# A fused attention, pooling and feed-forward kernel: finer waits and moved set-up in groups two to six, and a first group prepared by three engines

## The chip, the cores and the metric

The kernel runs on one core of a Trainium2 chip. The metric is the device time of one execution in microseconds (us). Three runs of the kernel before gave a median of 279.13 us (278.16 to 279.15).

## What is computed

The input is x, 64 sequences of 64 tokens with 256 features (4096 tokens). Cut to what matters:

```python
# 1. rotation of x by a ** dt and cos, sin of f * dt (one scalar dt per sequence)
xr = stack([c * x0 - s * x1, s * x0 + c * x1])
# 2. linear attention, 16 heads of 16, keys layer-normed, decay gamma = sigmoid(log_gamma)
q, k, v = split(xr @ W_qkv.T);  k = layernorm(k)
S = gamma * S + outer(v_t, k_t);  y_t = S q_t
x = x + y @ W_o.T
# 3. pooling: softmax over masked scores tanh(x W1 + b1) v; one of three masks per sequence
x_p = softmax(masked(scores)) @ x / count
# 4. feed-forward with fake-quantized activations and weights (I = 704)
scale_w = max(abs(w), axis=1) / 127
x = x + down(quant(silu(gate(quant(x_p))) * up(quant(x_p))))
```

The weight scales (largest entry of a row over 127, and its inverse) and the sigmoid of two clip factors are the set-up that the change moves.

## The kernel before

The 4096 tokens are cut into eight groups of 512 (`for g in range(G)`, g from 0 to 7). I call them groups 1 to 8. Each engine has its own hand-written instruction list, with counting semaphores between them; nothing is reordered, so an instruction that waits holds up everything behind it on its engine. After the eight groups, the feed-forward part follows for all tokens (from about 205 us); the change does not touch it.

**One group.** TensorE (block `pe`, line 872 on) computes `scores(g, 0)`, `project_v(g)`, the transposed rows of the group before (`x1_rows`), `scores(g, 1)`, then `weights_turn` (line 964 on; it transposes softmax weights of two groups before), `hidden_layer`, `pool_tokens`, `score_rows`, then the first `values_pair`, the K projection of the next group, `squares`, half of the Q projection, the other `values_pair`s, `sums_turn` (line 1061; it transposes the sums of squared keys), the other half of Q, and `project` for four token blocks, which multiplies y by the output weights. In the first two groups of tokens (c < TURNED) `weights_turn` waits for `p_ok`, that is for normalized softmax weights; later it waits for the exponents only.

VectorE (block `dve`, line 1332 on) runs per group: `decays(g, 0)` (L1460, four products of scores and decay factors), `scale_v` (L1530), `decays(g, 1)`, `softmax_scores` (L1540 to L1542), `largest_rows` (L1560), `softmax_weights` (line 1545 on: a sum L1547, a product of four numbers L1548, a reciprocal L1550 or L1552, and in the first two blocks a 128x256 product L1555), `y_odd(g, 0)` (L1475), `sums_copy(g + 1)` (L1418), `low_y(g, 0)` (L1480), then in groups 3 to 5 the weight scales (`gu_scales`, `down_scales`, lines 1443 to 1456: largest entries L1444, a scaling L1445, a reciprocal L1446) and in group 3 the clip factors (L1599, L1600), `y_odd(g, 1)`, `low_y(g, 1)`, `newton(g + 1)` (L1514 to L1519, eleven dependent steps for an inverse square root), and the two `residual`s (L1468). The first group's `sums_copy(1)` comes after `low_y(0, 1)`.

ScalarE copies results out of PSUM: `next_x` (L662), `x1_columns` (L667), `k_copies` (L638, L639), `y_even` (L651), `y_high` (L656), `q_copies` (L644). A half of y goes: values on TensorE, `y_even` on ScalarE, `y_odd` on VectorE, `y_high` on ScalarE, `low_y` on VectorE, `project` on TensorE.

GpSimd does, per group, `low_x(g + 1)` (L531, two 128x512 products, right after `next_x`), the rotation of the group after that (`rotate`, L517 to L525, six 128x512 products) and the masks (`allowed`, L546 to L551).

**Waits of the values projection.** `project_v(g)` of groups 2 to 8 waits, before anything, for the Newton steps and the first residual:

```python
if g:
    pe.wait_ge(rs_ok, g + 1)
    pe.wait_ge(x1_done, 2 * g - 1)
```

**The start.** The first group is prepared apart. VectorE computes the angles (L1357 to L1369), ScalarE their sines (L615, L616), GpSimd the powers `a_pow` (L504, first for 8 columns, then for 24). VectorE multiplies both to `cs` (L1385, L1386), rotates the first group in six 128x512 products (L1391 to L1401), centres the key weights (L1407), rounds them (L1408, `wT`, with the rest `wT_lo` in L1410), takes `xT_lo` (L1413) and the rests of the other weights (`low_weights`, L1422), multiplies the later columns of `cs` (L1426, L1427) and writes the decay exponents in sixteen operations (L1437), whose `dec_arg` releases ScalarE's exponential (L728) and GpSimd's `rotate(1)`. ScalarE computes exp and log for the decay rates (L620, L716), with two table loads, and rounds the query weights (L618). TensorE turns `cs` (L1108) ahead of the first half of Q, `squares(0, ...)`, and `sums_turn(0)`. `keep_clock` (L1030) are matmuls on constants without use for the result.

## Time and profile before

| what | us |
|---|---|
| median of three runs | 279.13 |
| profiled execution | 279.3 |
| its span | 277.6 |
| TensorE busy (share of the span) | 255.3 (92%) |
| VectorE busy | 232.6 (84%) |
| ScalarE busy | 180.6 (65%) |
| GpSimd busy | 145.2 (52%) |
| granted TensorE clock, all slices | 1.00 |

Busy time is what an engine spent on instructions; the span begins with the first and ends with the last instruction of the execution. In rows of the trace, PE is TensorE, PEld its weight loads, DVE VectorE, ACT ScalarE, POOL GpSimd. A row gives the start, the length and, in square brackets, how long the engine was idle before it and what it waited for. Matrix multiplications in FP32 count as two instructions there.

### The profile page before, as it was taken

What the parts mean: (1) busy time and instruction counts of PE and PEld (TensorE: products, weight loads), DVE (VectorE), ACT (ScalarE), POOL (GpSimd) and SP (SyncE); (2) the same over time, 40 slices, a digit from 0 to 9 for tenths busy, and PEclk for the clock granted to TensorE, in tenths of its full rate; (3) what the DMA queues carried; (4) which work ended last, traced back from release to release, by engine and by line L of the source; (5) the groups of instructions that cost most, each with busy time, mean ns of one, the idle gap of its engine ahead of it and who ended that gap; (6) DMA issues with size and microseconds to landing.
All of it is one profiled execution on the core that took longest, in us unless ns stands there. A gap on an engine that the chain in (4) does not pass through costs nothing.

```text
span 277.6 us, 8491 instructions
## 1 busy us (share of the span) xinstructions
PE 255.3 (92%) x3545; PEld 176.0 (63%) x3545; DVE 232.6 (84%) x501; ACT 180.6 (65%) x316; POOL 145.2 (52%) x140
## 2 busy tenths in 40 slices
PE   5898999988998899899899999998889999998995
PEld 5767769657877777777777886885634434433331
DVE  4999869479699878978987786787888999999994
ACT  2775481552467647768748547527689999847991
POOL 6939595990593278059339533003212679850570
PEclk9999999999999999999999999999999999999999
DMA  5990504400900530194084033040009489000167
GB/s 164 336 275 3 153 0 151 159 2 13 293 5 2 190 117 2 35 291 43 0 302 62 2 129 84 2 138 22 0 0 200 113 219 348 35 0 0 72 256 280
DMA packets 30311, 31.20 MB, mean 112 GB/s; under 512 B 12929, under 2 KB 20673, under 8 KB 30273
## 3 DMA queue, kind: packets, MB, share of 16 engines
q1 hardware_dynamic: 30272, 30.66, 37.2%
q8 instruction: 28, 0.46, 0.7%
q14 instruction: 11, 0.08, 0.1%
HBM read 19.48 MB, written 8.42 MB: 100 GB/s over the span
## 4 chain that ended last, share of the span: by engine, by line
PE 45%; DVE 32%; ACT 13%; issue 6%; DMA 1%; POOL 1%; DVEq 0%; ACTq 0%
PE psum L879 11%; PE psum L1271 6%; PE psum L904 4%; DVE yT_lo L1480 4%; PE psum L1290 3%; DVE psum L1475 3%; PE psum L986 3%; ACT silu L842 2%; PE psum L961 2%; ACT silu L824 2%; PE psum L1030 2%; DVE arena L1468 2%; PE psum L942 2%; PE psum L1023 2%; DVE arena L1651 2%
## 5 line engine op out<-in xcount | busy, mean ns | idle before, releaser
L1460 DVE TENSOR_TENSOR arena<-psum,xq_mem 128x512 f32<-128x512 f32 x64 | 39.7, 682 | 7.0 <-PE psum L904 7.0
L531 POOL TENSOR_TENSOR xT_lo<-arena,xT 128x512 fp32r<-128x512 f32 x14 | 18.0, 1308 | 46.1 <-ACT xT L662 46.1
L1271 PE MATMUL psum<-xq_mem,guT 128*128 128x512 bf16 x152 | 33.9, 380 | 0.2
L662 ACT ACTIVATE xT<-arena 128x512 fp32r<-128x512 f32 x14 | 8.1, 623 | 29.5 <-PE psum L879 26.0
L1271 PEld LDWEIGHTS psum<-xq_mem,guT 128*128 128x128 bf16 x152 | 14.4, 98 | 19.4 <-DVE arena L1651 1.8
L1662 DVE TENSOR_REDUCE h_max<-arena 128x1 f32<-128x1024 f32 (+1 forms) x24 | 25.9, 1123 | 0.2
L824 ACT ACTIVATE silu<-psum,gu_x 128x1024 f32<-128x1024 f32 (+1 forms) x24 | 24.4, 1025 | 2.1 <-PE psum L1271 1.1
L879 PE MATMUL psum<-wT,xT 128*128 128x256 f32 x64 | 17.3, 293 | 4.8 <-DVE arena L1468 4.8
L1475 DVE SCALAR_TENSOR_TENSOR psum<-psum,pmask,arena 128x256 f32<-128x256 f32 x28 | 12.3, 485 | 10.0 <-ACT arena L651 10.0
L904 PE MATMUL psum<-arena 32*64 32x128 f32 x1024 | 19.3, 278 | 1.1 <-issue 1.1
L644 ACT ACTIVATE arena<-psum,pmask 128x512 f32<-128x512 f32 x32 | 20.1, 684 | 0.1
L1290 PE MATMUL psum<-arena,dT 128*128 128x512 bf16 x80 | 18.9, 381 | 1.2 <-DVE arena L1721 0.6
L919 PE MATMUL psum<-arena 64*32 64x128 f32 x1024 | 19.5, 274 | 0.4 <-DVE arena L1460 0.4
L879 PE MATMUL psum<-woT,yT 128*128 128x256 f32 x64 | 17.2, 291 | 1.0 <-ACT yT L656 0.9
L919 PEld LDWEIGHTS psum<-arena 64*32 64x32 f32 x1024 | 13.9, 106 | 6.3 <-issue 6.3
L904 PEld LDWEIGHTS psum<-arena 32*64 32x64 f32 x1024 | 15.5, 131 | 3.7 <-issue 2.6
L598 POOL CAST arena<-silu 128x1024 bf16<-128x1024 int8 (+1 forms) x9 | 9.6, 1095 | 14.3 <-DVE silu L1716 13.1
L656 ACT ACTIVATE yT<-psum 128x256 fp32r<-128x256 f32 x28 | 10.7, 387 | 9.3 <-DVE psum L1475 9.2
L879 PE MATMUL psum<-wT_lo,xT 128*128 128x256 f32 x64 | 16.7, 282 | 0.0
L879 PE MATMUL psum<-woT_lo,yT 128*128 128x256 f32 x64 | 16.6, 282 | 0.0
L517 POOL TENSOR_TENSOR arena<-xin,cs_rows 128x512 f32<-128x512 f32 x7 | 9.4, 1342 | 13.8 <-DMA cs_rows<-cs_dram 9.0
L546 POOL TENSOR_TENSOR xq_mem<-kind,xq_mem 128x256 f32<-128x256 f32 x8 | 5.1, 635 | 21.8 <-DVE arena L1542 21.8
(251 smaller groups left out, 734.1 us busy)
## 6 DMA issues: line engine op xcount, KB each, us to landing
arena<-in_x SPq DMA_DIRECT2D x9, 512.0 KB, 3.8
x_dram<-arena SPq DMA_DIRECT2D x8, 512.0 KB, 4.1
pooled<-x_dram SPq DMA_DIRECT2D x8, 512.0 KB, 5.3
out<-pooled SPq DMA_DIRECT2D x15, 256.0 KB, 2.2
xin<-in_x_t SPq DMA_DIRECT2D x7, 512.0 KB, 4.5
cs_rows<-cs_dram SPq DMA_DIRECT2D x12, 256.0 KB, 5.2
pooled<-in_w_qkv_t SPq DMA_DIRECT2D x3, 256.0 KB, 4.9
pooled<-in_w_down SPq DMA_DIRECT2D x1, 704.0 KB, 7.4
```

What stands on the lines that cost most here:

```text
L531: pool.tensor_tensor(xT_lo[:, k, :], xrotT[:, k, :], xT[:, k, :].bitcast(F32), ALU.subtract).then_inc(xl_ok, 1)
L644: act.activation(qblk[:, c, odd, :], Q_BANK[c][:, :], ACT.Identity, scale=pmask[:, odd:odd + 1]).then_inc(q_ok, 1)
L824: act.activation(silu_tile(n, v)[:, a:], gate_bank(v)[:, a:], ACT.Silu, scale=gu_x[:, 0, v:v + 1]).then_inc(silu_ok, 1)
L879: return pe.matmul(o, w(k), x(k), start=start, stop=stop) if stationary_w else pe.matmul(o, x(k), w(k), start=start, stop=stop)
L904: mm = pe.matmul(bank[S_BANK[r]][S * b:S * b + S, p * P:p * P + P], kT[rows, c, t:t + S], qblk[rows, c, :, t:t + S], start=True, stop=True)
L919: last = pe.matmul(Y_BANK[half][b][32 * r:32 * r + 32, at_y:at_y + P], v_rows[rows, p, at_v:at_v + 32], dec[rows, c, r, p, :], start=True, ...
L1271: mm = pe.matmul(in_order(o[:, 512 * half:512 * half + 512], 2 * n + half), gT[i][:, v, c, :], xq_rows(2 * n + half, c), start=(c == 0), s ...
L1290: return pe.matmul(o, dT[:, c, v, :], hid_q[:, U * n + 2 * v + half, 0:512], start=first, stop=last)
L1460: dve.tensor_tensor(dec[:, c, r, :, :], bank[S_BANK[r]].rearrange("q (n k) -> q n k", n=PP), two_heads, ALU.mult).then_inc(dec_done, 1)
L1475: dve.scalar_tensor_tensor(o, y_psum(b, half, 1), pmask[:, 1:2], y_rows(b, half), ALU.mult, ALU.add).then_inc(y_ok, 1)
L1480: dve.tensor_tensor(y_part(yT_lo, b, half), y_full(g, b, half), y_part(yT, b, half).bitcast(F32), ALU.subtract).then_inc(yl_ok, 1)
L1662: dve.tensor_reduce(h_max[:, n, v:v + 1], hid_step(n, v), AX.X, ALU.max, apply_absolute_value=True).then_inc(hm_done, 1)
```

## The change

**Groups two to six.** `project_v` waits for `rs_ok` before its first half and for the first residual only before its second. `newton` can run in two parts: four steps after `low_y(g, 0)`, seven after `low_y(g, 1)`. `sums_turn` moves ahead of the second `values_pair`s, and `sums_copy` of groups 2 to 7 ahead of `y_odd(g, 0)`; in group 1 it moves ahead of `low_y(0, 1)`. `softmax_weights` is cut: the sum stays (`softmax_sums`), the rest goes to the next group, between `scale_v` and `decays(g, 1)`. The largest weight entries are taken one group earlier, between `sums_copy` and `y_odd(g, 0)` (groups 2, 3 and 4); the scales follow in groups 3, 4 and 5, and the clip factors in group 6, all of them between `scale_v` and `decays(g, 1)`.

**The first group.** ScalarE takes the absolute value, exp and log of the decay rates at once, ahead of the sines, and multiplies one half of each rotation product in eight 128x128 pieces; VectorE adds the other half in eight pieces, each with its own wait. GpSimd centres the key weights and rounds those of q and v. The decay exponents are two 128x512 products, from a table in which GpSimd has put 1e20 where no decay is wanted. GpSimd's `rotate(1)` no longer waits for `dec_arg`. The exponential of the decays is cut in two, between `q_copies`. TensorE turns `cs` after the first half of Q, and runs fewer `keep_clock` matmuls.

```diff
@@ TensorE @@
@@ def project_v(g)
                 pe.wait_ge(kT_ok, DC * g + DC)
-                if g:
-                    pe.wait_ge(rs_ok, g + 1)
-                    pe.wait_ge(x1_done, 2 * g - 1)
                 for j in (0, 1) if g else (1, 0):
-                    if g == 0 and j == 0:
-                        pe.wait_ge(rs_ok, 1)
+                    if j == 0:
+                        pe.wait_ge(rs_ok, g + 1)
+                    elif g:
+                        pe.wait_ge(x1_done, 2 * g - 1)
@@ the start
-            keep_clock(2, bank[3][:, 0:P], ident[:, :], ident[:, :])
...
-                keep_clock(4, bank[3][:, 0:P], ident[:, :], ident[:, :])
+                keep_clock(1, bank[3][:, 0:P], ident[:, :], ident[:, :])
...
+            pe.wait_ge(wl_ok, 1)
+            project_x(0, Q_BANK, 0, 0, q_mm)
             pe.wait_ge(cs_ok, 2)
             pe.wait_ge(csr_ok, 2)
             pe.transpose(bank[4][0:2 * NPAIR, 0:P], cs[:, :, :].rearrange("p k n -> p (k n)"), ident[:, :]).then_inc(cs_tr, 1)
-            pe.wait_ge(wl_ok, 1)
-            project_x(0, Q_BANK, 0, 0, q_mm)
@@ the groups
+                    if g:
+                        sums_turn(g + 1)
                     values_pair(1, 0)
                     values_pair(1, 1)
-                    if g:
-                        sums_turn(g + 1)
-                    else:
+                    if g == 0:
                         squares(1, 1)
@@ GpSimd @@
+            bounds(0)
             pool.wait_ge(ld_cols, 16)
             pool.wait_ge(ang_ok, 1)
+            powers(slice(0, 2 * PP))
+            pool.wait_ge(pow_ok, 1)
+            for b in range(2):
...
+                pool.affine_select(out=steps[half, :], in_=steps[half, :], compare_op=ALU.is_ge, fill=FAR, base=0,
...
+            pool.wait_ge(ld_k, 16)
+            pool.wait_ge(mean_ok, 1)
+            pool.tensor_tensor(centred.rearrange("p c (h d) -> p c h d", d=DK), raw_qkv[:, :, D:2 * D].rearrange("p c (h d) -> p c h d", d=DK),
+                               mean[:, :, :].unsqueeze(3).to_broadcast([P, DC, NH, DK]), ALU.subtract).then_inc(centred_ok, 1)
+            pool.wait_ge(ld_q, 16)
+            pool.tensor_copy(wT[:, 0, :, :], raw_qkv[:, :, 0:D]).then_inc(wqv_ok, 1)
+            pool.wait_ge(ld_v, 16)
+            pool.tensor_copy(wT[:, 2, :, :], raw_qkv[:, :, 2 * D:3 * D]).then_inc(wqv_ok, 1)
+            powers(slice(2 * PP, NPAIR))
@@ def rotate(g)
                 if g == 1:
                     pool.wait_ge(csr_ok, 2)
-                    pool.wait_ge(dec_arg, 1)
@@ ScalarE @@
-            act.wait_ge(ld_q, 16)
-            act.activation(wT[:, 0, :, :], raw_qkv[:, :, 0:D], ACT.Copy).then_inc(w_ok, 1)
...
+            act.wait_ge(ld_row, 16)
+            link(act.activation(lg[:, 1, :], lg_raw, ACT.Abs))
+            link(act.activation(lg[:, 2, :], lg[:, 1, :], ACT.Exp, scale=-1.0))
+            act.activation(lg[:, 3, :], lg[:, 2, :], ACT.Ln, bias=1.0).then_inc(lg_ln, 1)
             act.wait_ge(ang_ok, 2)
...
+            for h in range(2):
+                other = x1[1][:, :, HW:D] if h == 0 else x1[1][:, :, 0:HW]
+                for n in range(PP):
+                    act.activation(rot[:, h, n, :], other[:, n, :], ACT.Identity, scale=cs[:, 1, n:n + 1]).then_inc(rot_part, 1)
@@ VectorE, the start @@
-            dve.tensor_tensor(rot[:, 0, :, :], left, cos, ALU.mult)
-            dve.tensor_tensor(rot[:, 1, :, :], right, sin, ALU.mult).then_inc(dve_c, 1)
...
+                for n in range(PP):
+                    dve.wait_ge(rot_part, PP * h + n + 1)
+                    last = dve.scalar_tensor_tensor(xrot[:, n, cols], x1[1][:, n, cols], cs[:, 0, n:n + 1], rot[:, h, n, :], ALU.mult, sign)
...
-            for h in range(NH):
-                last = dve.scalar_tensor_tensor(decay[:, h, :], steps[:, :], lg[:, 4, h:h + 1], later[:, :], ALU.mult, ALU.add)
...
+                dve.tensor_tensor(decay[:, heads, :], steps[:, :].unsqueeze(1).to_broadcast([P, HC, S]),
+                                  lg[:, 4, heads].unsqueeze(2).to_broadcast([P, HC, S]), ALU.mult).then_inc(dec_arg, 1)
+            low_weights(1, raw_qkv[:, :, 2 * D:3 * D], wT[:, 2, :, :], wT_lo[:, 2, :, :])
             dve.wait_ge(pow_ok, 2)
             dve.tensor_tensor(cs[:, 0, rest], a_pow[:, rest], ang[:, 5, rest], ALU.mult).then_inc(cs_ok, 1)
             dve.tensor_tensor(cs[:, 1, rest], a_pow[:, rest], ang[:, 4, rest], ALU.mult).then_inc(cs_ok, 1)
...
             sums_copy(0)
@@ VectorE, the groups @@
                     scale_v(g, p)
+                if 2 <= g < G - 1:
+                    softmax_weights(c - 1)
+                if 2 <= g < 4:
+                    scales(g - 2, g_sc[:, g - 2, :], g_inv[:, g - 2, :], g_sc_ok[g - 2])
+                elif g == 4:
+                    scales(2, d_amax[:, 0, :], d_amax[:, 1, :], d_sc_ok)
+                elif g == 5:
...
                 decays(g, 1)
...
+                elif g:
+                    softmax_sums(c)
+                    sums_copy(g + 1)
+                    if g < 3:
+                        gu_largest(g - 1)
+                    elif g == 3:
+                        down_largest()
                     y_odd(g, 0)
...
                     low_y(g, 0)
+                    newton(g + 1, 0)
...
                 if g + 1 < G:
-                    newton(g + 1)
+                    newton(g + 1, 1 if g else None)
```

Two places of the order. **VectorE, group 3**, from its first decays to its softmax scores, before (`arena<-psum,xq_mem` are decays, `arena<-psum,rs` is the scaling of v, `sm_c` and `cnt` hold four numbers per row, `p_max` the largest pooled entries):

```order
L1460 TENSOR_TENSOR arena<-psum,xq_mem 128x512 [waits s_mm] x4
L1530 TENSOR_TENSOR arena<-psum,rs 128x256 [waits v_mm,rs_ok] x4
L1460 TENSOR_TENSOR arena<-psum,xq_mem 128x512 [waits s_mm] x4
L1540 TENSOR_TENSOR psum<-psum,xq_mem 128x256 [waits masks_on,sv_mm]
L1541 TENSOR_REDUCE sm_c<-psum 128x4 [waits cond_chain]
L1542 TENSOR_TENSOR arena<-psum,sm_c 128x256 [waits cond_chain]
L1560 TENSOR_REDUCE p_max<-pooled 128x1 [waits pl_cp]
L1547 TENSOR_REDUCE sm_c<-arena 128x4 [waits ex_ok]
L1548 TENSOR_TENSOR sm_c<-sm_c,cnt 128x4 [waits cond_chain]
L1552 RECIPROCAL sm_c<-sm_c 128x4 [waits cond_chain]
L1555 TENSOR_TENSOR arena<-arena,sm_c 128x256 [waits p_tr,cond_chain]
L1475 SCALAR_TENSOR_TENSOR psum<-psum,pmask,arena 128x4x64 [waits ye_ok] x2
```

and after, up to the softmax scores:

```order
L1461 TENSOR_TENSOR arena<-psum,xq_mem 128x512 [waits s_mm] x4
L1538 TENSOR_TENSOR arena<-psum,rs 128x256 [waits v_mm,rs_ok] x4
L1559 TENSOR_TENSOR sm_c<-sm_c,cnt 128x4 [waits cond_chain]
L1563 RECIPROCAL sm_c<-sm_c 128x4 [waits cond_chain]
L1566 TENSOR_TENSOR arena<-arena,sm_c 128x256 [waits cond_chain]
L1453 TENSOR_SCALAR g_sc<-g_sc 128x6 [waits amax_ok]
L1454 RECIPROCAL g_inv<-g_sc 128x6 [waits dve_chain]
L1461 TENSOR_TENSOR arena<-psum,xq_mem 128x512 [waits s_mm] x4
L1548 TENSOR_TENSOR psum<-psum,xq_mem 128x256 [waits masks_on,sv_mm]
L1549 TENSOR_REDUCE sm_c<-psum 128x4 [waits cond_chain]
L1550 TENSOR_TENSOR arena<-psum,sm_c 128x256 [waits cond_chain]
```

The product of four numbers, its reciprocal, the 128x256 product and the scaling of six numbers (`g_sc`) now stand between the scaling of v and the second decays; before, the first three stood behind the softmax scores.

**GpSimd, the start**, before (`a_pow` are powers, `xq_mem` bounds for the masks, `wT` rounded weights, `xin,cs_rows` the rotation of group 2):

```order
L504 TENSOR_TENSOR a_pow<-cols_sb,dt_b 128x8 [waits ang_ok,ld_cols]
L504 TENSOR_TENSOR a_pow<-cols_sb,dt_b 128x24
L556 AFFINE_SELECT xq_mem<-xq_mem 64x64
L558 AFFINE_SELECT xq_mem<-xq_mem 64x64 [waits pool_chain]
L560 AFFINE_SELECT xq_mem<-xq_mem 64x64 [waits pool_chain]
L556 AFFINE_SELECT xq_mem<-xq_mem 64x64 [waits pool_chain]
L558 AFFINE_SELECT xq_mem<-xq_mem 64x64 [waits pool_chain]
L560 AFFINE_SELECT xq_mem<-xq_mem 64x64 [waits pool_chain]
L562 TENSOR_TENSOR xq_mem<-xq_mem 128x64 [waits pool_chain]
L563 TENSOR_TENSOR xq_mem<-xq_mem 128x64
L566 CAST wT<-pooled 128x512 [waits ld_v]
L517 TENSOR_TENSOR arena<-xin,cs_rows 128x512 [waits rot_done,dec_arg,xl_ok,csr_ok,xin_in]
```

and after, behind the first powers (the first three bounds now stand ahead of those):

```order
L523 AFFINE_SELECT steps<-steps 64x64 [waits pow_ok]
L523 AFFINE_SELECT steps<-steps 64x64 [waits lg_ok]
L528 TENSOR_TENSOR arena<-pooled,mean 128x512 [waits mean_ok,ld_k,lg_ok]
L531 CAST wT<-pooled 128x512 [waits ld_q]
L533 CAST wT<-pooled 128x512 [waits ld_v]
L514 TENSOR_TENSOR a_pow<-cols_sb,dt_b 128x24
L505 AFFINE_SELECT xq_mem<-xq_mem 64x64 [waits pow_ok]
L507 AFFINE_SELECT xq_mem<-xq_mem 64x64 [waits pool_chain]
L509 AFFINE_SELECT xq_mem<-xq_mem 64x64 [waits pool_chain]
L585 TENSOR_TENSOR xq_mem<-xq_mem 128x64 [waits pool_chain]
L586 TENSOR_TENSOR xq_mem<-xq_mem 128x64
L546 TENSOR_TENSOR arena<-xin,cs_rows 128x512 [waits rot_done,xl_ok,csr_ok,xin_in]
```

The centring and two roundings now stand ahead of the second powers, and those ahead of the second bounds; the rotation's first product waits no more for `dec_arg`.

## Rows read from the trace of the kernel before

**Rows 1.** Stretches: us, busy us (count) of PE, PEld, DVE, ACT, POOL; clock, DMA share, GB/s.
```profile
26.40:48.20 21.80, 20.70 (x372) 17.17 (x371) 17.84 (x46) 9.20 (x20) 15.11 (x14) 1.00 0.29 91
48.20:71.41 23.21, 20.48 (x378) 16.08 (x380) 17.05 (x42) 10.54 (x24) 12.99 (x13) 1.00 0.27 89
71.41:95.77 24.36, 22.41 (x412) 18.26 (x414) 21.13 (x48) 15.82 (x33) 12.81 (x13) 1.00 0.28 90
95.77:119.53 23.76, 22.54 (x412) 18.40 (x415) 19.46 (x45) 15.84 (x33) 12.77 (x13) 1.00 0.25 93
119.53:141.72 22.19, 21.20 (x395) 16.80 (x397) 19.19 (x45) 15.56 (x32) 12.79 (x13) 1.00 0.51 110
141.72:163.19 21.47, 21.22 (x396) 16.80 (x398) 17.14 (x42) 12.46 (x28) 12.78 (x13) 1.00 0.39 109
163.19:184.64 21.45, 21.21 (x396) 16.81 (x397) 16.81 (x42) 12.08 (x27) 5.09 (x6) 1.00 0.26 70
```

**Rows 2.** PE's waits over the run: us in total, times, longest us.
```profile
PE psum L879 <- DVE arena L1468: 4.8, 6, 1.1
PE psum L1063 <- DVE sq_sums L1418: 2.7, 3, 1.4
```

**Rows 3.** Timeline, group 3's set-up: start us, us, engine, line, operation.
```profile
83.64 1.74 DVE L1444 TENSOR_REDUCE g_sc<-pooled 128x6 f32<-128x1536 f32 x1
85.41 0.59 DVE L1445 TENSOR_SCALAR g_sc<-g_sc 128x6 f32<-128x6 f32 x1
85.24 0.73 POOL L551 TENSOR_TENSOR xq_mem<-xq_mem 128x256 f32<-128x256 f32 x1
```

**Rows 4.** Timeline, VectorE beside GpSimd in group 3.
```profile
79.24 1.28 POOL L522 TENSOR_TENSOR arena<-xin,cs_rows 128x512 f32<-128x512 f32 x1
79.44 1.11 DVE L1548 TENSOR_TENSOR sm_c<-sm_c,cnt 128x4 f32<-128x4 f32 x1
80.48 1.28 POOL L523 TENSOR_TENSOR arena<-xin,cs_rows 128x512 f32<-128x512 f32 x1
80.79 1.26 DVE L1555 TENSOR_TENSOR arena<-arena,sm_c 128x256 f32<-128x256 f32 x1
```

**Rows 5.** Timeline around the second score block of group 4.
```profile
94.55 1.41 DVE L1530 TENSOR_TENSOR arena<-psum,rs 128x256 f32<-128x256 f32 x4
95.70 2.51 POOL L531 TENSOR_TENSOR xT_lo<-arena,xT 128x512 fp32r<-128x512 f32 x2 [9.73 <-ACT xT L662]
96.84 0.44 PE L977 MATMUL psum<-ident,arena 128*128 128x128 f32 x2
```

**Rows 6.** Timeline, group 5: second decay block and the values after it.
```profile
120.65 2.48 DVE L1460 TENSOR_TENSOR arena<-psum,xq_mem 128x512 f32<-128x512 f32 x4 [0.94 <-PE psum L904]
123.64 0.67 PE L919 MATMUL psum<-arena 64*32 64x128 f32 x32
```

**Rows 7.** Timeline, group 2: the even and odd halves of y.
```profile
56.46 0.82 ACT L651 ACTIVATE arena<-psum,pmask 128x256 f32<-128x256 f32 x2
59.31 0.87 DVE L1475 SCALAR_TENSOR_TENSOR psum<-psum,pmask,arena 128x256 f32<-128x256 f32 x2
```

**Rows 8.** Timeline, the start: the first group's preparation.
```profile
6.24 4.16 POOL L504 TENSOR_TENSOR a_pow<-cols_sb,dt_b 128x24 f32<-128x24 f32 x1
8.17 0.69 DVE L1391 TENSOR_TENSOR arena<-arena,cs 128x512 f32<-128x512 f32 x1
8.29 1.28 ACT L620 ACT_TABLE_LOAD   x1
15.92 0.17 DVE L1427 TENSOR_TENSOR cs<-a_pow,ang 128x24 f32<-128x24 f32 x1
16.65 3.22 DVE L1437 SCALAR_TENSOR_TENSOR xq_mem<-steps,lg,later 128x64 f32<-128x64 f32 x16
20.09 1.72 POOL L517 TENSOR_TENSOR arena<-xin,cs_rows 128x512 f32<-128x512 f32 x1 [4.73 <-issue]
27.59 2.48 DVE L1460 TENSOR_TENSOR arena<-psum,xq_mem 128x512 f32<-128x512 f32 x4 [0.26 <-PE psum L904]
```

203 lines of the change are left out of this document (97 added, 106 removed).

## The prediction

> **What bounds the kernel now.** I number the eight groups of 512 tokens 1 to 8 (the loops' g is one less). I read first the busy time by stretch, cut at the second block of scores of each group [rows 1]: TensorE is idle for 1.1, 2.7, 1.95, 1.2, 1.0, 0.25 and 0.25 us of the stretches of groups 1 to 7. So the groups are TensorE's own work plus small waits, 8.5 us in all, and no edit there can bring more. Its waits say where they lie [rows 2]: for the first residual (L1468), and for the copy of the sums of squares (L1418). The steady stretch (group 7) is 21.45 us; groups 3 to 5 are longer since VectorE prepares the weight scales there: 1.74 us for the largest entries and 0.59 us for a product of six numbers [rows 3], ahead of the second half of y. To the values block of group 1 nothing repeats; there it is a chain through all engines.
>
> **What decides the changed order.** The third view is VectorE beside GpSimd. A product of 4 numbers (L1548) took 1.11 us: it began at 79.44 and ended at 80.55, as GpSimd's L522 ended (80.52). L1555 was held until the end of L523 (81.76) and was through 0.29 us later [rows 4]. The product of six numbers ended as L551 did [rows 3]. So a VectorE operation with two SBUF inputs, or an SBUF-to-SBUF scaling, waits for the running GpSimd product, and then gets in before the next one.
>
> **Groups 2 to 7, term by term** (gain positive; each against the idle time of its stretch [rows 1]).
> - Group 1's end. `sums_copy(1)` now stands before `low_y(0, 1)`. Before, the transposition of the sums waited 0.7 us for it with all projections behind it. That goes, and the values projection of group 2 waits no more for the first residual: **+0.65**. I price the end of the waits at this and not at 1.1, as the rest is the wait for decays in this stretch, which stays.
> - Group 2. The 1.4 us for the copy and the 1.1 us for the residual [rows 2] go. But y's odd half can't follow at once: its even half was ready at 57.3, VectorE came at 59.31 [rows 7], behind 2.4 us of softmax weights. These move to group 3, yet the 1.74 us for the largest gate entries move in, from 57.3 to 59.05. So y is only 0.25 us earlier, and TensorE, which now comes 1.4 us sooner to the third projection, waits 1.1 us there for yT. Net of both waits: **+1.45**.
> - Group 3. `softmax_weights(0)` now stands between the scaling of v and the second decays. In group 4, where the rows stand for both, v is scaled until 95.96, and GpSimd's two `low_x` products run from 95.70 to 98.21 [rows 5]. The 4-number product is held to the end of the first (about 97.0), the reciprocal follows, the 128x256 product is held to 98.21 and ends 0.29 later, at 98.5. Its result is what TensorE's turn of the weights waits for, and TensorE came to that at 96.84 [rows 5]: a new stall of 1.65 us, with the hidden layer, pooling and scores behind it. Further on the largest entries (1.74 us) stand ahead of y's first half, right behind the squares: yT of the second half comes 0.4 us after TensorE wants it. 22.4 busy + 2.05 is the old 24.36: **-0.05**. The old waits (copy, scales, residual) are all gone, which is why it isn't worse.
> - Group 4: the same stall of 1.65, and 0.25 for y (1.61 us of reduction): 22.5 + 1.9 = 24.4 against 23.76, **-0.6**.
> - Group 5: no matrix product waits for softmax weights here, but the scaling of two numbers behind them is held to the end of the second `low_x` product, 121.97 by the pattern of group 4, and the decays start at 122.2 instead of 120.65. They need 2.48 us and end at 124.7; TensorE wants them at 123.64 [rows 6]. Stall 1.05 for an idle time of 0.99: **-0.05**.
> - Group 6: the same through the two clip numbers, now moved here: 1.05 for 0.25, **-0.8**.
> - Group 7: only the weights move, the decays start 0.25 us late, inside their slack of 0.5; the early part of the Newton steps takes the wait for the residual away: **+0.25**. Group 8: nothing.
> Sum **+0.85**. The Newton split itself costs nothing: four steps of 0.27 us lie in VectorE's wait of 1.1 us for y's second even half, and if that cover were gone, the residual would be late next, which now only the second half of the values projection waits for. The transposition of the sums, moved ahead of the values pair, costs 0.1 us of TensorE at the same total. Of the DMA queues none is passed by a moved step; the joined semaphore of the small loads delays nothing, as no wait for one of them shows in the trace.
> The Trainium skill ("SBUF — State Buffer", section "Who interferes with whom") has the same lock: a VectorE instruction with two SBUF inputs contends with a GpSimd instruction that reads SBUF, and the loser blocks for the whole instruction. [Rows 3] and [rows 4] agree with it, but [rows 8] do not: see the last rival.
>
> **The start, up to the first group's second decays** (27.59 + 2.48 = 30.07 [rows 8]).
> - Taken off VectorE: six 0.69 us products of the rotation (eight pieces of about 0.3 us now, each behind a ScalarE piece of about 0.3, by L651's two pieces in 0.82 us [rows 7] and half their width), the centring (0.7), and sixteen decay operations, 3.22 us, which become two of 0.69. Sum about 3 us off VectorE; the copy of w_q (0.6) goes from ScalarE to GpSimd.
> - Added: ScalarE loads three tables before the sines, two of them 1.28 us each [rows 8] after the logs; the first lies under the wait for data. From the landing of the row at 4.1 us: three small activations (0.22 each) and two loads give the sines at 7.8, the time at which VectorE used them anyway (7.9). Covered, by 0.1 us. Eight of the matmuls that keep TensorE's clock go; TensorE waits for the rotation there, so they cost and save nothing while the granted clock stays at 1.00 [rows 1].
> - GpSimd's centring (a 1.28 us product) starts at 7.6, with the means. VectorE's cosines and sines (128x8, two SBUF inputs) come at 7.8 and are held to 8.9: 0.9 us late, 1.4 if the second is held by the cast of w_q behind it. The rotation's shorter end gives this back: rot_done at 11.9 to 12.5 for 12.1. The weights and xT_lo are 0.3 to 0.8 us earlier.
> - Then GpSimd's second powers (4.16 us) end at 14.3 for 10.4, bounds and the group-2 rotation follow at once, as the wait for `dec_arg` is gone. VectorE has five operations with two SBUF inputs there: two decay products, w_v's rest, and the pair of late cosines, which was done at 16.09 [rows 8] and whose turning on TensorE stands ahead of squares, sums and Newton. That such meetings cost is seen at L517, 1.72 us for 1.27 [rows 8]. If the rotation begins behind w_v's rest, the pair is held once, by one product of 1.28 us: ready at 19.35.
> - From that pair to the end of the second decays: turning 0.3, squares 0.65, half of q 0.8, sums and Newton 3.0, decays 2.4, scaling 1.4, decays 2.5, together 11.05. 19.35 + 11.05 = 30.4: **-0.4**. Bounds: the pair passes ahead of the rotation, ready at 17.9 and 29.1 by q and Newton, **+0.9**; the rotation begins under the first decay product and alternates with all five, ready at 22: **-3.1**. I take the nearer end's neighbour, as in [rows 4] a waiting VectorE operation lost one GpSimd product and no more.
>
> **Sum.** +0.85 - 0.4 = 0.45 us less than the profiled execution's 279.3 (its span is 277.6, 1.7 us lie around it): 278.85. That execution stands 0.17 us above the median of the three runs, so the forecast is **278.7 us**. A change of 0.5% (1.4 us) is about what a measurement of this kernel can tell from none.
>
> **Rivals.**
> - *The early waits cost nothing* (0.15). If the moved weights slip in before `low_x`, or GpSimd's first product comes later, the stalls of groups 3 to 6 vanish and only y's 0.4 and 0.25 stay: +4.0 there, with +2.1 from groups 1 and 2 and +0.9 at the start 272.1. For it: v's last scaling ended just 0.26 us after `low_x` began [rows 5]. Against: both start from the same event, so that distance should stay.
> - *Half the collisions miss* (0.27). The start goes by its good bound (277.4 alone), or the two-number scalings of groups 5 and 6 aren't held (1.9 us less, 276.8 alone), or both (275.5). For it: only six-number scalings were seen clearly held.
> - *The start alternates* (0.21, slower). VectorE and GpSimd take turns through all five operations, the cosines are ready at 22 and 281.4 is the result. It decides from a readiness of 21.2 us on, where the loss at the start passes 2.25 us. For it: without the wait for `dec_arg` GpSimd's products are always ready; against: GpSimd must first finish bounds, which VectorE's products hold up.
> - *Everything that reads SBUF locks out* (0.03, slower). Then the second powers would hold VectorE's rotation pieces from 10.2 to 14.3, some 3 us, and give 282. In this trace they did not: L1391 ran in 0.69 us under a power operation from 6.24 to 10.40 [rows 8], and its neighbours in the same. The Trainium skill's section named above would have it so, since both read SBUF.
> My forecast (the moved work meets GpSimd's products, and the waits only change place) has 0.34. It is also the case in which the change doesn't do what it says: waits are finer, but not shorter.
>
> **Numbers.** Faster by over 0.5%: 0.15 + 0.27 = 0.42; within: 0.34; slower: 0.24. The range of 8 in 10 runs from 273.0, which leaves out most of the first rival, to 281.5. The forecast's own range is 277.4 to 280.
>
> **What would show it.** The 4-number product of groups 3 to 7 at about 1 us, directly behind v's scaling; TensorE idle for about 1.65 us before the turn of the weights in groups 3 and 4, and for 1 us before the values of groups 5 and 6; no wait for the first residual; the stretches of groups 1 to 7 at 21.1, 21.8, 24.4, 24.4, 22.2, 22.3, 21.2; the first group's second decays ending near 30.4. Stretches of 22.8, 22.8, 21.2 and 21.2 in groups 3 to 6 would prove me wrong about the lock, an end of those decays beyond 32 wrong about the start.

## The result, and the profile after

| | before | after |
|---|---|---|
| median of 20 executions, us | 279.74 | 275.93 |
| their range, us | 278.16 to 280.90 | 275.58 to 281.81 |
| profiled execution, us (its span) | 279.3 (277.6) | 275.67 (273.9) |

The change makes the kernel 1.06% faster: ratio 0.9894, 95% interval 0.9872 to 0.9916. The ratio leaves out the four executions of 280.49 to 281.81 us, which had the lowest TensorE clock (a mean of 0.976 to 0.982), and keeps the five of 278.7 to 278.8 us, so it isn't the quotient of the medians. The two profiled executions are 3.6 us apart. The forecast was 278.7 us; the time lies inside the range of 273.0 to 281.5, but beyond the 0.5% line that the forecast stayed within.

The same stretches as in [rows 1], from one group's second block of scores to the next one's, in the profile of the changed kernel (groups 1 to 7, columns as there):

```profile
24.30:45.76 21.46, 20.91 (x372) 17.31 (x372) 17.08 (x48) 9.21 (x20) 13.73 (x13) 1.00 0.27 87
45.76:67.31 21.55, 20.41 (x370) 16.07 (x369) 16.38 (x40) 10.47 (x24) 12.77 (x12) 1.00 0.28 97
67.31:91.79 24.48, 22.45 (x405) 18.25 (x404) 20.26 (x47) 15.82 (x33) 12.71 (x12) 1.00 0.27 88
91.79:116.17 24.38, 22.48 (x404) 18.25 (x403) 20.12 (x47) 15.82 (x33) 12.71 (x12) 1.00 0.28 90
116.17:138.47 22.30, 21.29 (x388) 16.92 (x387) 18.72 (x45) 15.71 (x32) 12.75 (x12) 1.00 0.47 124
138.47:159.70 21.23, 21.23 (x388) 16.90 (x388) 17.68 (x45) 12.59 (x28) 12.77 (x12) 1.00 0.37 100
159.70:180.92 21.22, 21.22 (x388) 16.89 (x388) 16.59 (x43) 12.22 (x27) 5.16 (x6) 1.00 0.27 70
```

The second block of scores of group 1 begins at 24.30 us for 26.40. But part of that is only where the cut lies: the block now has to wait, bank by bank, for VectorE's first decays, and takes 1.67 us for 1.2. The end of the second decays (26.02 + 2.48 = 28.50 for 30.07) is the fair cut. The gains (positive is faster), in us:

| | start | group 1 | 2 | 3 | 4 | 5 | 6 | 7 | rest |
|---|---|---|---|---|---|---|---|---|---|
| forecast | -0.4 | +0.65 | +1.45 | -0.05 | -0.6 | -0.05 | -0.8 | +0.25 | 0 |
| measured | +1.57 | +0.87 | +1.66 | -0.12 | -0.62 | -0.11 | +0.24 | +0.23 | -0.02 |

They sum to the 3.7 us between the spans. Two terms are wrong, the start by 2.0 us and group 6 by 1.0 us.

TensorE's waits in the changed kernel, from the same view as [rows 2]:

```profile
PE psum L999 <- DVE arena L1566: 3.3, 2, 1.6
PE psum L901 <- ACT yT L683: 1.6, 3, 0.9
PE psum L941 <- DVE arena L1461: 1.5, 2, 1.0
```

The 7.5 us for the residual and for the copy of the sums [rows 2] are gone. In their place stand 3.3 us for the moved softmax weights (L1566; groups 3 and 4), 1.6 us for the high part of y (groups 2 to 4, behind the largest entries; 0.9 us before) and 1.0 us for group 5's second decays; 0.48 us of the last row is group 1's. By the stretches above, TensorE is idle for 0.55 us less in group 1 and 1.6 us less in group 2 than before, but no less in groups 3 and 5 and 0.7 us more in group 4: there the waits were only exchanged.

VectorE beside GpSimd in groups 4, 5 and 6 (L560 is `low_x`, L1559 the product of four numbers, L1453 and L1590 the scalings of two numbers, L1461 the decays, L1538 the scaling of v; the second decays are the rows at 118.83 and 140.01):

```profile
91.79 2.50 POOL L560 TENSOR_TENSOR xT_lo<-arena,xT 128x512 fp32r<-128x512 f32 x2 [9.46 <-ACT xT L689]
92.04 1.04 DVE L1559 TENSOR_TENSOR sm_c<-sm_c,cnt 128x4 f32<-128x4 f32 x1
93.33 1.24 DVE L1566 TENSOR_TENSOR arena<-arena,sm_c 128x256 f32<-128x256 f32 x1
94.62 0.44 PE L999 MATMUL psum<-ident,arena 128*128 128x128 f32 x2 [1.63 <-DVE arena L1566]
...
116.42 1.06 DVE L1559 TENSOR_TENSOR sm_c<-sm_c,cnt 128x4 f32<-128x4 f32 x1
117.72 0.98 DVE L1453 TENSOR_SCALAR d_amax<-d_amax 128x2 f32<-128x2 f32 x1
118.83 2.46 DVE L1461 TENSOR_TENSOR arena<-psum,xq_mem 128x512 f32<-128x512 f32 x4
...
134.59 2.48 DVE L1461 TENSOR_TENSOR arena<-psum,xq_mem 128x512 f32<-128x512 f32 x4 [0.28 <-PE psum L926]
136.99 1.54 DVE L1538 TENSOR_TENSOR arena<-psum,rs 128x256 f32<-128x256 f32 x4
138.45 0.15 DVE L1559 TENSOR_TENSOR sm_c<-sm_c,cnt 128x4 f32<-128x4 f32 x1
138.48 2.50 POOL L560 TENSOR_TENSOR xT_lo<-arena,xT 128x512 fp32r<-128x512 f32 x2 [7.09 <-ACT xT L689]
138.85 0.92 DVE L1590 TENSOR_SCALAR clip_s<-clip_s 128x2 f32<-128x2 f32 x1
140.01 2.48 DVE L1461 TENSOR_TENSOR arena<-psum,xq_mem 128x512 f32<-128x512 f32 x4
```

In group 4 a product of 4 numbers takes 1.04 us and ends at 93.08, 0.04 us after GpSimd's first product (half of 2.50 us from 91.79 on). In group 6 the same operation began 0.03 us before GpSimd's and took 0.15 us; only the scaling behind it was held, so the decays began 1.54 us after the second block of scores and not 2.66 us, as in group 5.

The start, in the same view as [rows 8]:

```profile
7.88 0.95 DVE L1398 TENSOR_TENSOR cs<-a_pow,ang 128x8 f32<-128x8 f32 x1 [0.30 <-ACT ang L648]
9.90 4.20 POOL L514 TENSOR_TENSOR a_pow<-cols_sb,dt_b 128x24 f32<-128x24 f32 x1
12.29 0.69 DVE L1413 TENSOR_TENSOR wT_lo<-arena,wT 128x512 fp32r<-128x512 f32 x1
14.17 0.71 POOL L505 TENSOR_SCALAR_AFFINE_SELECT xq_mem<-xq_mem 64x64 f32<-64x64 f32 x1
15.15 1.33 DVE L1434 TENSOR_TENSOR xq_mem<-steps,lg 128x512 f32<-128x512 f32 x2
16.63 0.76 POOL L586 TENSOR_TENSOR xq_mem<-xq_mem 128x64 f32<-128x64 f32 x1
17.14 0.29 DVE L1438 TENSOR_TENSOR cs<-a_pow,ang 128x24 f32<-128x24 f32 x1
17.35 1.30 POOL L546 TENSOR_TENSOR arena<-xin,cs_rows 128x512 f32<-128x512 f32 x1
17.35 0.17 DVE L1439 TENSOR_TENSOR cs<-a_pow,ang 128x24 f32<-128x24 f32 x1
18.52 0.29 DVE L1421 TENSOR_SCALAR sq_sums<-psum 128x128 f32<-128x128 f32 x1 [1.00 <-PE psum L1077]
26.02 2.48 DVE L1461 TENSOR_TENSOR arena<-psum,xq_mem 128x512 f32<-128x512 f32 x4
```

L1438 and L1439 are the pair of late cosines. The second of them begins in the same hundredth of a microsecond as GpSimd's rotation (L546) and isn't held. The pair is ready at 17.52 us, and 11.0 us later the second decays end. The copy of the sums (L1421) comes at 18.5 us; before, it stood behind the sixteen decay operations, which ended at 19.87 [rows 8].

### The profile page after: what moved, and what is told of

Same layout as the page of the kernel before. It is cut to its first block, busy times and chain, and to the rows that moved or that the text cites. A ratio compares the mean times of both kernels' runs of the same rounds, so it can differ in the third digit from the quotient of the medians.

```text
span 273.9 us, 8463 instructions
## 1 busy us (share of the span) xinstructions
PE 254.1 (93%) x3529; PEld 174.6 (64%) x3529; DVE 226.4 (83%) x483; ACT 183.3 (67%) x325; POOL 145.9 (53%) x144
## 4 chain that ended last, share of the span: by engine, by line
PE 53%; DVE 26%; ACT 12%; issue 5%; DMA 1%; POOL 1%; DVEq 0%; ACTq 0%
PE psum L901 10%; PE psum L1290 6%; DVE arena L1461 5%; PE psum L941 4%; PE psum L1309 3%; PE psum L926 3%; PE psum L1062 3%; ACT silu L864 2%; PE psum L1008 2%; PE psum L1068 2%; PE psum L1063 2%; PE psum L1064 2%; PE psum L1069 2%; ACT silu L846 2%; PE psum L1051 2%
## 5 line engine op out<-in xcount | busy, mean ns | idle before, releaser
L1461 DVE TENSOR_TENSOR arena<-psum,xq_mem 128x512 f32<-128x512 f32 x64 | 39.6, 681 | 3.8 <-PE psum L926 3.7
L560 POOL TENSOR_TENSOR xT_lo<-arena,xT 128x512 fp32r<-128x512 f32 x14 | 17.5, 1273 | 45.4 <-ACT xT L689 45.4
L846 ACT ACTIVATE silu<-psum,gu_x 128x1024 f32<-128x1024 f32 (+1 forms) x24 | 24.4, 1026 | 2.1 <-PE psum L1290 1.1
L901 PE MATMUL psum<-wT,xT 128*128 128x256 f32 x64 | 17.5, 296 | 0.0
L1675 DVE TENSOR_TENSOR arena<-psum,silu 128x1024 f32<-128x1024 f32 (+1 forms) x13 | 14.7, 1136 | 1.8 <-ACT silu L846 1.8
```

The costliest lines, as they stand in the source:

```text
L560: pool.tensor_tensor(xT_lo[:, k, :], xrotT[:, k, :], xT[:, k, :].bitcast(F32), ALU.subtract).then_inc(xl_ok, 1)
L846: act.activation(silu_tile(n, v)[:, a:], gate_bank(v)[:, a:], ACT.Silu, scale=gu_x[:, 0, v:v + 1]).then_inc(silu_ok, 1)
L901: return pe.matmul(o, w(k), x(k), start=start, stop=stop) if stationary_w else pe.matmul(o, x(k), w(k), start=start, stop=stop)
L1461: dve.tensor_tensor(dec[:, c, r, :, :], bank[S_BANK[r]].rearrange("q (n k) -> q n k", n=PP), two_heads, ALU.mult).then_inc(dec_done, 1)
L1675: dve.tensor_tensor(hid_step(n, v)[:, a:], up_bank(v)[:, a:], silu_tile(n, v)[:, a:], ALU.mult).then_inc(h_ok, 1)
```

## Experiments

**The two parts of the change, each alone.** `groups_alone` is the kernel before with the edits of the groups' loop, `newton`, `project_v` and `sums_turn`; `start_alone` is the changed kernel with exactly these taken back.

> The kernel before with the groups' part of the change alone (finer waits, moved set-up work); the start is left as it was. Theory: the two parts are independent. The stretches of groups 2 to 7 measured 1.3 us shorter in sum in the changed kernel and group 1's 0.3 us, so this kernel takes 1.6 us off the 279.3 us of the profiled execution: 277.7 us, ratio 0.994, with the same waits of 1.6 us for L1566 in groups 3 and 4 and of 1.0 us for the decays in group 5. Rival: the gain at the start is partly the groups' (the copy of group 2's sums moved ahead of the low part of y), then this one gives 2.5 us or more, ratio 0.991 or less.

Measured: 278.15 us, ratio 0.9935 (0.9899 to 0.9971). Its second blocks of scores begin at 26.44, 47.41, 68.98, 93.45, 117.81, 140.15, 161.41 and 182.63 us: 2.0 us ahead of before at the end, of which 0.83 in group 1. TensorE waits 3.3 us for L1566 in two pieces here too. The profiled execution took 277.39 us, 0.3 us less than expected; four of the eight took 278.79 us or more.

> The kernel before with the first group's part alone; the groups are left as they were. Theory: the start is worth what the second block of scores of group 1 shows, 24.3 us for 26.4 us: 2.1 us, so 277.2 us, ratio 0.9925, and the late cosines are ready near 17.5 us as in the changed kernel. Rival: the head start is lost in group 1, which has its own wait for the sums (0.7 us): then 0.5 us at most remains, ratio 0.998.

Measured: 278.07 us, ratio 0.9933 (0.9911 to 0.9954). The late cosines are ready at 17.72 us and the second decays end at 28.70, 1.37 us earlier than before; 1.35 us of it is left at the second block of scores of group 8 (183.29 for 184.64). So the parts are nearly independent: 2.0 and 1.35 us make 3.35 of the 3.7; where the other 0.35 us come from was not looked for. The time is 0.9 us above the 277.2 expected: I had taken 2.1 us for the start, and that was the cut described above.

**GpSimd steps aside in groups 3 to 6.**

```diff
 def low_x(g):
+    if g - 1 in (2, 3):
+        pool.wait_ge(g_sc_ok[g - 3], 1)
+    elif g - 1 == 4:
+        pool.wait_ge(d_sc_ok, 1)
+    elif g - 1 == 5:
+        pool.wait_ge(clip_ok, 1)
```

(`clip_ok` is a new semaphore on the reciprocal of the clip numbers.)

> The changed kernel, but GpSimd begins the low part of x (2.5 us, two products) in groups 3 to 6 only after VectorE's moved set-up work is done. Theory (a GpSimd product holds VectorE's operations with SBUF inputs): the product of 4 numbers falls from 1.05 to 0.15 us, L1566 from 1.24 to 0.3, the two-number scaling from 0.98 to 0.15; TensorE's two waits of 1.6 us for L1566 and that of 1.0 us for group 5's decays go; the low part of x ends some 0.9 us later, which TensorE doesn't see, since it uses it 5.9 us after its end in group 4. 275.7 - 4.3 = 271.4 us, ratio to the kernel before 0.972. Rival (the operations are slow for a reason of their own, or the weights are late whatever GpSimd does): durations stay at 1.0 and 1.2 us, the time is 275.7 or up to 1 us above, ratio 0.987 to 0.991.

Measured: 271.29 us, ratio 0.9687 (0.9667 to 0.9708). The same place in group 4, VectorE, TensorE and GpSimd by start time:

```profile
90.40 0.15 DVE L1565 TENSOR_TENSOR sm_c<-sm_c,cnt 128x4 f32<-128x4 f32 x1
90.81 0.43 DVE L1572 TENSOR_TENSOR arena<-arena,sm_c 128x256 f32<-128x256 f32 x1
91.29 0.44 PE L1005 MATMUL psum<-ident,arena 128*128 128x128 f32 x2
91.62 2.50 POOL L566 TENSOR_TENSOR xT_lo<-arena,xT 128x512 fp32r<-128x512 f32 x2 [9.54 <-DVE g_inv L1460]
```

The product of 4 numbers takes 0.15 us, the 128x256 product 0.43 (I had said 0.3), and TensorE's matrix products don't wait for it (its weight load does, 0.17 us). The waits added to GpSimd take 4.4 us off the 275.7 us. That GpSimd's products hold VectorE up (I call this the lock) is the cause of these three stalls.

**The moved work at the head of the group**, where GpSimd is idle, with no wait added (the scales and the clip numbers move with the weights):

```diff
 for g in range(G):
...
+    if 2 <= g < G - 1:
+        softmax_weights(c - 1)
...
     decays(g, 0)
     for p in range(PP) if g else (2, 3, 0, 1):
         scale_v(g, p)
-    if 2 <= g < G - 1:
-        softmax_weights(c - 1)
...
     decays(g, 1)
```

> The changed kernel, but the moved softmax weights, weight scales and clip numbers of groups 3 to 7 stand at the head of the group, ahead of the first decays, where GpSimd has been idle for 7 to 9.5 us in the profile. No wait is added to GpSimd. Theory (the lock): all the short operations take 0.15 to 0.3 us, the three waits of TensorE (1.6, 1.6 and 1.0 us) go; the first decays start 0.65 to 1.1 us later, within the 0.98 us that lay in group 4 between their end and the second block of scores. 275.7 - 4.3 + 0.2 = 271.6 us, ratio 0.972. Rival (VectorE's order costs more than the lock): the later first decays hold back the second block of scores by 0.5 to 1 us in each of five groups, and 274 to 276 us is left, ratio 0.981 to 0.988.

Measured: 271.41 us, ratio 0.9691 (0.9670 to 0.9711), the same as with GpSimd's wait. Groups 3 to 6 take 22.86, 22.71, 21.22 and 21.22 us for 24.48, 24.38, 22.30 and 21.23.

**The largest entries into VectorE's own waits**, on top of that:

```diff
+if g == 1:
+    gu_largest(0)
 if g:
     softmax_scores(c)
...
     softmax_sums(c)
-    sums_copy(g + 1)
-    if g < 3:
-        gu_largest(g - 1)
+    if g == 2:
+        gu_largest(1)
     elif g == 3:
         down_largest()
+    sums_copy(g + 1)
     y_odd(g, 0)
```

> The kernel with the moved weights and scales at the head of the group, and in addition the largest entries moved into VectorE's own waits: for the gate ahead of group 2's masked scores (VectorE idle for 2.9 us there, the weights landed long before), for the other two ahead of the copy of the sums of squares (idle for 1.95 us in groups 3 and 4; the reductions take 1.74 and 1.61). Theory: TensorE's three waits for yT (0.9, 0.4 and 0.3 us) go and nothing takes their place: 271.4 - 1.6 = 269.8 us, ratio 0.9635. Rival (the copy of the sums is late next, or the hold-up only moves to y's odd half): 271 us or more, ratio 0.968 and up.

Measured: 269.16 us, ratio 0.9599 (0.9556 to 0.9642). The gain was 2.25 us where I had expected the 1.6 us of the waits. The last experiment's profile, below, has the same groups: groups 2, 3 and 4 are 1.15, 0.66 and 0.52 us shorter, and in each TensorE's busy time too is 0.25 us less for the same matmuls, which I had not counted and can't explain.

**Forcing the meeting at the start.** GpSimd's bounds and subtractions behind the rotation:

```diff
 pool.wait_ge(pow_ok, 2)
+rotate(1)
+pool.wait_ge(rot_done, 2)
 bounds(1)
 pool.tensor_tensor(base[:, 3, :], ...)
 pool.tensor_tensor(base[:, 4, :], ...)
-rotate(1)
```

> The changed kernel with GpSimd's last three bounds and two subtractions (3.2 us, 14.1 to 17.4) moved behind the rotation for group 2, which so starts at 14.3 us, when the rows of cosines are copied, and meets VectorE's five operations with two SBUF inputs (two products of the decays, the rest of w_v, the pair of late cosines). This is the case that my prediction gave its forecast and its third rival to. If VectorE loses one GpSimd product and then runs through: the pair is ready at 18.4 us for 17.5, the first group's second decays end at 29.4, the time is 276.6 us, ratio 0.990. If the two engines take turns through all five: the pair is ready near 22.2 us, the decays end at 33.2, the time is 280.4 us, ratio 1.003. If there is no lock here: 17.5 and 275.7 us, ratio 0.987.

Measured: 283.52 us, ratio 1.0122 (1.0065 to 1.0179), slower than before. VectorE and GpSimd, by start time:

```profile
14.45 1.47 POOL L546 TENSOR_TENSOR arena<-xin,cs_rows 128x512 f32<-128x512 f32 x1 [0.36 <-ACT cs_rows L743]
14.68 1.27 DVE L1429 SCALAR_TENSOR_TENSOR lg<-row_sb,lg 128x16 f32<-128x16 f32 x1
15.88 1.29 POOL L547 TENSOR_TENSOR arena<-xin,cs_rows 128x512 f32<-128x512 f32 x1
15.98 1.22 DVE L1430 TENSOR_SCALAR lg<-lg 128x16 f32<-128x16 f32 x1
17.24 2.36 DVE L1434 TENSOR_TENSOR xq_mem<-steps,lg 128x512 f32<-128x512 f32 x2
17.25 1.80 POOL L549 TENSOR_TENSOR arena<-arena 128x512 f32<-128x512 f32 x1
19.52 1.74 DVE L1425 TENSOR_TENSOR wT_lo<-pooled,wT 128x512 fp32r<-128x512 f32 x1
20.68 1.70 POOL L552 TENSOR_TENSOR arena<-xin,cs_rows 128x512 f32<-128x512 f32 x1
21.19 1.24 DVE L1438 TENSOR_TENSOR cs<-a_pow,ang 128x24 f32<-128x24 f32 x1
```

The engines take turns from 14.68 us on: a VectorE operation waits for a GpSimd product, and the next product for a VectorE operation. Two operations on 16 numbers, 0.2 us each, take 1.27 and 1.22 us. The pair is ready at 22.52 us. That is the third rival's readiness of 22 us, but the time is 3.1 us over the 280.4 us expected for it. TensorE's windows show a part of the reason (columns as in [rows 1]):

```profile
18.00:22.00 4.00, 0.00 (x0) 0.00 (x0) 4.00 (x3) 0.00 (x0) 3.92 (x3) 1.00 0.38 128
22.00:26.00 4.00, 3.43 (x22) 2.34 (x23) 0.97 (x4) 1.93 (x4) 2.96 (x7) 0.57 0.05 12
```

TensorE was idle for 5.3 us before it turned the cosines, and from 22 to 26 us its granted clock was 0.57, mostly the lower level of 1.2 GHz. From the pair to the end of the first group's second decays it took 12.3 us in place of 11.0; and group 1 is 1.4 us longer, 1.26 us of it a wait for the copy of group 2's sums. With the 0.3 us by which the pair is later than expected these are the 3.1 us.

**Two edits of the start undone**, first with the race against GpSimd's rotation left open:

```diff
 for c in range(DC):
-    dve.tensor_tensor(decay[:, heads, :], steps..., lg[:, 4, heads]..., ALU.mult)
+    for h in range(HC * c, HC * c + HC):
+        last = dve.tensor_scalar(decay[:, h, :], steps[:, :], lg[:, 4, h:h + 1], None, ALU.mult)
```

> The changed kernel with the arguments of the decays formed head by head again, in sixteen operations of 128x64 in place of two of 128x512. Sixteen took 3.22 us before, two take 1.33 us: 1.9 us more on VectorE ahead of the late cosines. Theory (the start is VectorE's chain up to the cosines, and it gained since the pair was ready before GpSimd's rotation began at 17.35 us): the pair comes at 19.4 us at least and is held by one or two products of 1.28 us: 20 to 21.5, the time is 278.2 to 279.5 us, ratio 0.995 to 1.000. Rival (the start is bounded by TensorE or by the second powers): under 0.5 us more, 276.2 us at most, ratio 0.989.

Measured: 286.93 us, ratio 1.0251 (1.0189 to 1.0313). Far more than I had expected; VectorE and GpSimd:

```profile
15.42 9.12 DVE L1434 TENSOR_SCALAR xq_mem<-steps,lg 128x64 f32<-128x64 f32 x16
16.59 1.28 POOL L546 TENSOR_TENSOR arena<-xin,cs_rows 128x512 f32<-128x512 f32 x1
```

Sixteen scalings took 9.12 us, until the rotation's six products were through at 24.33 us: six of them took 1.26 to 1.32 us, the other ten 0.24 to 0.36. TensorE waited 7.8 us for the pair (ready at 25.33), and its granted clock was 0.50 from 22 to 26 us. The profiled execution is the longest of the four (289.32 us); its clock was at 0.50 once more from 107 to 113 us, and its group 4 took 27.45 us for 24.38. So a part of this execution's time was lost far behind the start (see the last section).

The second edit takes ScalarE's pieces out:

```diff
-act.activation(rot[:, h, n, :], other[:, n, :], ACT.Identity, scale=cs[:, 1, n:n + 1]).then_inc(rot_part, 1)
...
-last = dve.scalar_tensor_tensor(xrot[:, n, cols], x1[1][:, n, cols], cs[:, 0, n:n + 1], rot[:, h, n, :], ALU.mult, sign)
+dve.tensor_tensor(rot[:, 0, :, :], left, one, ALU.mult)
+link(dve.tensor_tensor(rot[:, 1, :, :], right, two, ALU.mult))
+dve.tensor_tensor(xrot[:, :, HW * h:HW * h + HW], rot[:, 0, :, :], rot[:, 1, :, :], sign).then_inc(half, 1)
```

> The changed kernel with the first group's rotation on VectorE alone again, as six products of 128x512, and no piece of it on ScalarE. Theory: the rotation is done at 13.0 to 14.1 us for 11.9 (six times 0.69 us from 8.9 us on, with up to 1.1 us lost to GpSimd's two copies of weights), all of VectorE's chain is as much later, and the late cosines may in addition be held once by the rotation for group 2: the time is 276.8 to 279 us, ratio 0.991 to 0.999. Rival (the rotation wasn't on the chain, since K's projection waits for the weights): under 0.4 us more.

Measured: 285.93 us, ratio 1.0193 (1.0134 to 1.0251): pair ready at 23.47 us. The granted clock was 0.57 from 14 to 18 us, behind waits of 1.7 and 1.2 us for the rotated rows, and fell again at 24 us, behind 3.1 us of waiting for the pair. Both kernels show that an edit that costs 1 or 2 us on VectorE can cost 10 here, once the late cosines fall under the rotation; the lower clock is a part of the 10. They don't show the price of the edits themselves.

**The same with the order held.** One line more, in `rotate`, which takes the race away:

```diff
 if g == 1:
     pool.wait_ge(csr_ok, 2)
+    pool.wait_ge(cs_ok, 2)
```

> The changed kernel with one wait given back: GpSimd's rotation for group 2 starts only when both late cosines are done (before, it waited for the decays' arguments). Theory: in the changed kernel the rotation began at 17.35 us and the pair was ready at 17.52, so the order is the same already; the rotation begins 0.25 us later, which nothing sees (its result is used by ScalarE from 25.3 us on): 275.7 us, ratio 0.986, and the time spreads less. Rival (dropping that wait is what brought the gain at the start): 277.3 us or more, ratio 0.992 and up.

Measured: 275.75 us, ratio 0.9877 (0.9833 to 0.9922). The rotation begins at 17.71 us for 17.35, and all stretches are the same within 0.05 us. Since this wait ends later than that for `dec_arg` would (the second decay product is done at 16.44 us here), dropping the wait for `dec_arg` brought nothing. That the time would spread less did not come true: two of its six executions took 278.7 us.

> The kernel with the decays' arguments formed head by head (286.9 us), with the rotation for group 2 waiting for the late cosines. Theory (its 11 us were the lock, sixteen scalings each behind a product, and TensorE's clock that fell while TensorE waited 7.8 us): the sixteen take some 3.2 us in place of 9.1, the pair is ready at 19.4 to 19.9 us for 17.5, the granted clock stays at 1.00, the time is 277.6 to 278.2 us, ratio 0.993 to 0.995. Rival (the scalings are slow by themselves, 0.57 us each): 286 us again. If the clock also falls at an idle time of 2.2 us of TensorE, 1.3 us more than the theory's.

Measured: 279.03 us, ratio 0.9947 (0.9910 to 0.9983). The sixteen scalings take 2.89 us, the pair is ready at 18.84 us, the second decays end at 29.83: 1.3 us is what the two wide operations are worth against this form. The time is above the 277.6 to 278.2 us expected. Its ten executions lie between 277.05 and 283.29 us, and the lowest is 1.5 us above the lowest of the changed kernel (275.58); the rest is the subject of the last section.

> The kernel with the first group's rotation on VectorE alone (285.9 us), with the rotation for group 2 waiting for the late cosines. Theory: the pieces on ScalarE are worth the 1.7 us by which the rotation ended later (13.65 for 11.9 us), no more; the other 8 us were the alternation with GpSimd and the clock. Pair ready at 19.2 us, time 277.4 to 278 us, ratio 0.992 to 0.994, if the clock holds. If the clock falls at 14 us already, where TensorE waits for the rotated rows (0.57 in that kernel from 14 to 18 us), 1 to 2 us more.

Measured: 278.28 us, ratio 0.9950 (0.9913 to 0.9987). Pair ready at 19.22 us, second decays done at 30.19: the pieces on ScalarE are worth 1.7 us at the start, as expected, though the time is 0.3 us above the range given. The clock held at the start here, with the same waits of 1.7 and 1.2 us for the rotated rows. The start's gain rests on the work taken off VectorE, by both edits. Together they make 3.0 us, more than the 1.57 us gained, so the rest of the start's change cost something or the two overlap; no run separates that.

**All together**: head of the group, largest entries in the waits, and the rotation's wait.

> The kernel with weights and scales at the head of the group and the largest entries in VectorE's waits (269.2 us), with the rotation for group 2 waiting for the late cosines. Theory: 269.1 us, ratio 0.960, in every run within 0.3 us, since no order at the start is left to a race of 0.2 us. Rival (the later rotation is seen in group 1): 269.6 us or more.

Measured: 269.00 us (268.94 to 269.20 in six executions), ratio 0.9604 (0.9580 to 0.9629), against 0.9877 (0.9833 to 0.9922) for the version with the same start and the groups as changed:

```profile
45.73:66.13 20.40, 20.15 (x370) 16.02 (x369) 16.79 (x43) 10.48 (x24) 12.78 (x12) 1.00 0.32 106
66.13:88.33 22.20, 22.20 (x405) 18.29 (x404) 18.98 (x47) 16.00 (x33) 12.76 (x12) 1.00 0.33 110
88.33:110.52 22.19, 22.19 (x405) 18.28 (x404) 18.58 (x46) 15.99 (x33) 12.78 (x12) 1.00 0.27 98
110.52:131.74 21.22, 21.22 (x389) 16.89 (x388) 16.46 (x43) 15.73 (x32) 12.77 (x12) 1.00 0.46 116
```

These are groups 2 to 5. TensorE is idle for 0.25 us in group 2 and not at all from there to group 8. In the changed kernel it was idle for 1.1 us in group 2, 2.0 and 1.9 us in groups 3 and 4, and 1.0 us in group 5.

## Why the prediction was right or wrong

**Right: the lock, its places and its sizes.** The 4-number product takes 1.04 to 1.06 us behind v's scaling in groups 3, 4 and 5; TensorE waits 1.63 us for the weights in groups 3 and 4 (1.65 forecast) and 1.0 us for the values of group 5. Groups 3 to 5 came out at 24.48, 24.38 and 22.30 us (24.4, 24.4 and 22.2). Two kernels that take the meeting away in different ways give 271.3 and 271.4 us. The Trainium skill ("SBUF — State Buffer", section "Who interferes with whom") says that whoever issues first has the shared ports for the whole instruction; the 0.03 us of group 6 and the turns in `rotation_first` agree with it.

**Right: groups 1 and 2**, each 0.2 us better than said (with group 1 cut at the end of the second decays). In group 2 TensorE waits 0.9 us for yT where I had 1.1.

**Wrong: group 6** ("the same through the two clip numbers", -0.8, measured +0.24). The step that failed is the one that carried the distance of group 4 over: v's scaling was to end 0.26 us after GpSimd's start. In groups 3 to 5 VectorE comes to its first decays straight from the residuals, and v's scaling ended 0.32 to 0.34 us after `low_x` began; in group 6 VectorE is early enough that its first decays wait for TensorE (0.28 us), and v's scaling is through as `low_x` begins (138.53 and 138.48 us). The 4-number product slips in first. My second rival had the outcome that the scalings of groups 5 and 6 aren't held. Neither came true: group 5's took 0.98 us and group 6's 0.92. Group 6 gained since the product ahead of its scaling wasn't held, so that the scaling lost `low_x`'s first product and not its second.

**Wrong: the start** (-0.4, measured +1.57). The chain from the pair of late cosines on was right (11.05 us said, 11.0 measured). The mis-sized term is when the pair is ready: 19.35 us by me, 17.52 us measured. I had the rotation begin behind w_v's rest and hold the pair for one product. That product never came between: w_v's rest ended at 17.22 us, the first cosine began at 17.14, and the rotation only at 17.35 us, since GpSimd's three bounds and two subtractions ahead of it took from 14.17 to 17.39 us, beside VectorE's products. With VectorE out of the way the same five take 1.5 us in `rotation_first` (0.24 for a bound and 0.32 for a subtraction, where L505 takes 0.71 and L586 0.76 here). I had named this as the argument against the third rival and left it out of the sum. The good bound fell short by 0.6 us as well (decays done at 28.50 us for 29.1): 0.4 of it is the pair, at 17.5 for 17.9. A small slip besides: 30.4 for 30.07 is -0.33, where the sum took -0.4.

**The third rival** (0.21) did not happen, but `rotation_first` shows it exists: pair at 22.5 us, slower than before. How near the changed kernel is to it isn't known: the second cosine and the rotation begin together, at 17.35 us here and at 17.55 in `start_alone`, and neither profile shows a cosine held by the rotation. Its readiness of 22 us was right and its price too low, by the clock and by group 1's wait.

**The fourth rival** is refuted: under the second powers (9.90 to 14.10 us) VectorE's product L1413 took 0.69 us, like its neighbours. So the rule of the Trainium skill in that section, by which any GpSimd instruction that reads SBUF contends, isn't borne out for the power operation; for bounds, subtractions and products it is.

The forecast case, "waits only change place", holds for groups 3 to 5 alone. The 0.42 for a gain of over 0.5% was where the outcome lay; I had given the largest single chance, 0.34, to the sum, and both of its errors made it too slow. The nearest case in number was the second rival's with both of its halves (275.5 us, for 275.67 profiled), and that is luck: its second half did not happen as told, and what it lacked there the start and groups 1 and 2 gave.

## What to carry to other kernels

An operation of 0.15 us that has its inputs in SBUF cost up to a whole GpSimd product (0.9 to 1.3 us) where it was moved next to one: before moving small set-up work, look at what GpSimd is running at the new place, not at how idle VectorE is there. The same work moved some 4 us further up, into a stretch where GpSimd waits, was worth 4.3 us; and a long reduction belongs into a wait that the engine has anyway. Where two engines may meet within a fraction of a microsecond, a semaphore can fix the order: here it cost nothing (275.75 us for 275.93) and took 8 us off each of the two kernels in which they met (286.93 to 279.03, 285.93 to 278.28).
